# The gate block goes whole ahead of the sum of squares, and half of the key/value batch moves to the odd steps

## The chip, the cores and the metric

One core of a Trainium2 chip runs the whole program in one launch. The metric is the device time of that core in microseconds (us). Two times are told from each other by the median of several executions.

## The reference

A transformer block on 4 sequences of 256 rows and 512 channels, float32. Cut to what matters here:

```
h = layernorm(x) * (1 + ca) + sa
q, k = rope(h @ Wq.T), rope(h @ Wk.T)          # 32 heads of q, 8 of k and v, D = 128
v    = h @ Wv.T
dt = softplus(h @ Win.T + dt_bias); g = -dt * exp(A_log_bias)
# chunks of 128 rows, G = cumsum(g) in a chunk
y = (q k^T * exp(G_i - G_j), causal) @ (v dt)  +  (q exp(G)) @ state
y = y / sqrt(mean(y^2) + 1e-5) * gnorm_w
y = y * silu(h @ Wg.T)
x = x + ga * (y @ Wo.T)
x = x + gb * ffn(layernorm(x) * (1 + cb) + sb)  # silu(h Wg) * (h Wu), then Wd
```

## The kernel before

Float32 values are split into a high and a low part, and each product is three matmuls (`three_products`, L69 to L73: high x high, high x low, low x high). All engines are programmed by hand, each with its own instruction list; semaphores (`wait_ge`, `then_inc`) are the only order between them. Nothing is scheduled by a tool.

The attention runs over 8 key/value groups g, and in each over 8 steps t. Step t handles chunk c = t % 2 of sequence b = t // 2 (two chunks of 128 rows a sequence), for the four heads of the group at once. A loop holds the groups 0 to 6, and the last group is written out: its steps 0 to 3 like the loop's, its steps 4 to 7 by `tail`. Each step also computes a part of what comes later: the q projection and the gate projection of one head for half of all rows (`q_block`, `g_block`, 12 matmuls of 512 columns each), and in even steps (c = 0) the key/value projection of the next sequence, both chunks (`kv_batch`, 24 matmuls of 256 columns into the bank `ps_kv`).

TensorE's order in a step (`step`, L717 to L734): scores of the chunk (`ps_s`); `q_block`; the output product of the step before (`ps_o`, waits for `z_hi` and `z_lo`); in odd steps the transposes of k into `ps_kv` (`k_turn`, L581); y (`ps_y`, in odd steps ahead of it four products with the state, L695); in even steps the chunk's state (`ps_st`, L706); `g_block` but for its last three matmuls; the sum of squares over the head, a product of ones with `sq_hi` (L712) and with `sq_lo` (L714) into `ps_ss`; the last three gate matmuls; in even steps `kv_batch`.

What the others do around it. ScalarE (ACT), in this order: `prob_hi`; two copies of `ps_q` into `q_sin` (L778, L779); the squares of y into `work` (L877) and `sq_hi` (L878); the copy of the state or, in odd steps, of kT (L820); four exponentials of `dec`; `rms` from `ps_ss` (L888, L891); the exponential of the gate (L783); `z_hi`; two more for the gate; in even steps `v`, `v_hi` (L815, L816) and the exponential `qe` (L796) of the next sequence's decays. VectorE (DVE), in this order: `probabilities` into `work` (L1206, waits for `z_lo` of the step before and for the scores); in odd steps `rotate_k` (L996 to L1002, writes `kr`); the gate `sg` (L1029); `prob_lo`; `q_cos` (L1009); in steps 1 to 4 the high parts of the next group's weights of one head; `qT` (L1017); the sum `x` (L1035); `sq_lo` (L1223); y times gate (L1226); a low part; y times `rms` (L1233); `cap` (L1023); a low part; `z_lo`. In step 0 `wo_hi` and, at the end, `wo_lo` are split too, in step 5 the key/value weights. GpSimd (POOL): `q_sin` times the sine (L1342); in odd steps `v_lo`, `vw`, `qe`; in even steps the causal mask on the next sequence's decays (L1335, waits for ScalarE's `qe`). SyncE (SP) issues the loads of the next group's weights and decays, behind `wh_split`, `wo_split`, `kv_split` and `prob_done`, which VectorE increments.

`work` is one buffer for the probabilities, the squares, and z, so `probabilities` of a step can't start ahead of `z_lo` of the step before.

Of the kernel before, what the change touches and what calls it, by code (L numbers as in the profile page):

```python
# [1 line left out]

# [9 lines left out]
B, L, HID = 4, 256, 512  # L29
# [5 lines left out]
KT = HID // P  # L35
NT = B * L // P
CPB = L // CHUNK
# [31 lines left out]
def three_products(pe, out, w_hi, w_lo, x_hi, x_lo, first, last):  # L69

    pe.matmul(out, w_hi, x_hi, start=first, stop=False)  # L71
    pe.matmul(out, w_hi, x_lo, start=False, stop=False)  # L72
    return pe.matmul(out, w_lo, x_hi, start=False, stop=last)  # L73
# [138 lines left out]
def block_attention(nc, cst, x1, hT_hi, hT_lo, tok, modT, gnorm, ident, modrow, gT_dram,  # L212
                    x_in, cT_in, wmod_in, wq_in, wg_in, wkv_in, wo_in, win_in, rows_in,
                    gnorm_in, cst_in, wgu_in, norm_rows, raw_pair):
    with ExitStack() as ctx:
# [6 lines left out]
        def sem(name):  # L222
            return ctx.enter_context(nc.semaphore(name))
# [99 lines left out]
        kv_ready = sem("kv_ready")  # L323
# [211 lines left out]
        def _(pe):  # L535
            def q_block(g, t, first=False):

                half, j = (t // 4 + 1) % 2, t % 4
                gw = g + 1 if t >= 4 else g
                pe.wait_ge(wh_split, gw * 4 + (j + 1))  # L540
                if not first:
                    pe.wait_ge(qcos_done, g * 8 + (t + 4))
                for k in range(KT):
                    cut = slice(half * HALF, (half + 1) * HALF)
                    last = three_products(nc.tensor, ps_q[:], wq_hi[:, j, k], wq_lo[:, j, k],
                                          hT_hi[:, k, cut], hT_lo[:, k, cut], k == 0, k == KT - 1)
                last.then_inc(q_ready, 1)

            def g_block(g, t, k_from, k_to, first=False):

                half, j = (t // 4 + 1) % 2, t % 4
                if k_from == 0 and not first:
                    pe.wait_ge(sg_done, g * 8 + (t + 4))
                for k in range(k_from, k_to):
                    cut = slice(half * HALF, (half + 1) * HALF)
                    last = three_products(nc.tensor, ps_g[:], wg_hi[:, j, k], wg_lo[:, j, k],
                                          hT_hi[:, k, cut], hT_lo[:, k, cut], k == 0, k == KT - 1)
                if k_to == KT:
                    last.then_inc(g_ready, 1)

            def kv_batch(g, b):

                bn = (b + 1) % B
                gw = g + 1 if b == B - 1 else g
                pe.wait_ge(kv_split, gw + 1)
                if b >= 0:
                    pe.wait_ge(kT_done, g * 4 + (b + 1))
                for c in range(CPB):
                    cut = slice((bn * CPB + c) * P, (bn * CPB + c + 1) * P)
                    for k in range(KT):  # L570
                        last = three_products(nc.tensor, ps_kv[:, c * 2 * D:(c + 1) * 2 * D],
                                              hT_hi[:, k, cut], hT_lo[:, k, cut],
                                              wkv_hi[:, k], wkv_lo[:, k], k == 0, k == KT - 1)
                last.then_inc(kv_ready, 1)

            def k_turn(g, b):

                pe.wait_ge(kr_done, g * 4 + (b + 2))
                pe.wait_ge(v_done, g * 4 + (b + 2))
                for c in range(CPB):  # L580
                    last = nc.tensor.transpose(ps_kv[:, c * P:(c + 1) * P], kr[:, c], ident)  # L581
                last.then_inc(kt_ready, 1)

            def out_product(g, t):

                pe.wait_ge(zhi_done, g * 8 + (t + 1))
                pe.wait_ge(zlo_done, g * 8 + (t + 1))
                if t <= 1:
                    pe.wait_ge(wo_split, g + (t + 1))
                for h in range(GRP):  # L590
                    last = three_products(nc.tensor, ps_o[:], z_hi[:, h], z_lo[:, h],
                                          wo_hi[:, h], wo_lo[:, h], h == 0, h == GRP - 1)
                last.then_inc(o_ready, 1)
# [62 lines left out]
            for t in range(1, 6):  # L656
                norm.tensor_turn(pe, t)
            pe.wait_ge(norm.lo_done, CPB)
            kv_batch(0, -1)
            norm.tensor_turn(pe, 6)  # L660
            norm.tensor_turn(pe, 7)
# [13 lines left out]
            cumulative()  # L675
            q_block(0, -1)
            g_block(0, -1, 0, KT)

            def scores(g, t):

                b, c, half = t // 2, t % 2, t // 4
                pe.wait_ge(kT_done, g * 4 + (b + 1))
                pe.wait_ge(rope_done, g * 8 + (4 * half + 4))
                nc.tensor.matmul(ps_s[:].rearrange("p (h i) -> p h i", h=GRP),  # L684
                                 kT[:, b % 2, c * P:(c + 1) * P], qT[:, half, :, rows_of(t)],
                                 start=True, stop=True).then_inc(s_ready, 1)

            def y_product(g, t):

                b, c = t // 2, t % 2  # L690
                if c == 1:
                    pe.wait_ge(qe_done, g * 4 + (b + 1))
                    pe.wait_ge(state_done, g * 4 + (b + 1))
                    for h in range(GRP):
                        nc.tensor.matmul(ps_y[:, h * P:(h + 1) * P], state[:, h], qe[:, b % 2, h],  # L695
                                         start=h == 0, stop=False)
                pe.wait_ge(vlo_done, g * 4 + (b + 1))
                pe.wait_ge(plo_done, g * 8 + (t + 1))
                p_hi, p_lo = (p[:].rearrange("p h i -> p (h i)") for p in (prob_hi, prob_lo))
                three_products(nc.tensor, ps_y[:], v_hi[:, b % 2, c], v_lo[:, b % 2, c], p_hi, p_lo,  # L700
                               c == 0, True).then_inc(y_ready, 1)

            def chunk_state(g, b):

                pe.wait_ge(vw_done, g * 4 + (b + 1))
                nc.tensor.matmul(ps_st[:].rearrange("p (h e) -> p h e", h=GRP), kr[:, 0],  # L706
                                 vw[:], start=True, stop=True).then_inc(st_ready, 1)

            def square_sum(g, t):

                pe.wait_ge(sqhi_done, g * 8 + (t + 1))
                nc.tensor.matmul(ps_ss[:], ones[:], sq_hi[:], start=True, stop=False)  # L712
                pe.wait_ge(sqlo_done, g * 8 + (t + 1))
                nc.tensor.matmul(ps_ss[:], ones[:], sq_lo[:], start=False, stop=True)\  # L714
                    .then_inc(ss_ready, 1)

            def step(g, t, project, next_batch, next_group):  # L717
                b, c = t // 2, t % 2
                scores(g, t)
                if project:  # L720
                    q_block(g, t)
                out_product(g, t)
                if c == 1 and next_batch:
                    k_turn(g, b)
                y_product(g, t)
                if c == 0:
                    chunk_state(g, b)
                if project:
                    g_block(g, t, 0, KT - 1)
                square_sum(g, t)  # L730
                if project:
                    g_block(g, t, KT - 1, KT)
                if c == 0 and next_batch:
                    kv_batch(g, b)  # L734

            def tail(g, t):
                b, c = t // 2, t % 2
                if t == 4:
                    scores(g, t)
                    mod_row(GA)  # L740
                    out_product(g, t)
                if c == 1:
                    pe.wait_ge(prob_done, g * 8 + (t + 1))
                y_product(g, t)
                if c == 0:
                    chunk_state(g, b)
                    scores(g, t + 1)
                if t == 4:
                    kv_batch(g, b)
                else:  # L750
                    pe.wait_ge(lnss_done, g * 8 + t)
                if t == 5:
                    k_turn(g, b)
                    pe.wait_ge(guard, 2)
                    mod_row(CB)
                if t == 7:
                    mod_row(GB)
                square_sum(g, t)
                if t == 5:
                    scores(g, t + 1)  # L760
                if t > 4:
                    out_product(g, t)
                if t == 5:
                    mod_row(SB)
                if t == 7:
                    mod_turn(ps_late_modT, late_rows, 4)
# [989 lines left out]
```

## Time and profile before

| | us |
|---|---|
| executions | 1148.46, 1152.65, 1151.79 |
| median | 1151.79 |
| the profiled execution: time | 1148.5 |
| the profiled execution: span | 1148.5 |
| one group of eight steps in the loop | 106.6 |
| an even step | 14.1 |
| the odd steps 1, 3, 5, 7 | 13.3, 12.5, 12.4, 11.9 |

The steps are taken from one scores row (L684) to the next in the timeline. "Waited for" in square brackets behind a row is the idle time of that engine ahead of the instruction, and what released it. Matmuls overlap: what one costs in a stream is the distance between starts, not the time that its row gives.

### The profile page before, as it was taken

How to read it: one execution, taken by the hardware profiler on the slowest of the kernel's cores; microseconds unless marked ns; L12 is line 12 of the kernel's file. 1: busy time of each engine (PE TensorE's matmuls, PEld its weight loads, DVE VectorE, ACT ScalarE, POOL GpSimd, SP SyncE). 2: the span in 40 equal slices, each digit the busy share in tenths (PEclk: the TensorE clock that was granted, in tenths of full speed). 3: DMA queues.
4: the chain of work that ended last, by engine and by line, in shares of the span. 5: the costliest groups of instructions: out<-in, count | busy, mean ns of one | idle time of the engine just before them, and what ended most of it. 6: DMA issues, size and time to landing. Idle time of an engine off the chain costs nothing. (4 is left out here: it accounts for less than half of the span.)

```text
span 1148.5 us, 14892 instructions
## 1 busy us (share of the span) xinstructions
PE 1076.9 (94%) x4936; PEld 835.7 (73%) x4936; DVE 848.1 (74%) x1432; ACT 612.4 (53%) x1257; POOL 328.7 (29%) x227
## 2 busy tenths in 40 slices
PE   4879999999999999999999999999999869999898
PEld 2657778777777777777777777777776348888676
DVE  5768887988788788879877887888787786434311
ACT  3445666666566666666666656666665434222300
POOL 3423333333433333333333333333332630000000
PEclk9989999999999999999999999999999989999899
DMA  6121301220131013112201310131031422111011
GB/s 216 56 69 56 116 22 37 73 73 18 37 110 37 18 37 120 35 41 76 74 18 37 110 37 18 37 110 37 21 105 32 173 88 78 55 37 55 28 37 37
DMA packets 37466, 70.90 MB, mean 62 GB/s; under 512 B 2937, under 2 KB 19577, under 8 KB 35521
## 3 DMA queue, kind: packets, MB, share of 16 engines
q1 hardware_dynamic: 36720, 70.16, 19.3%
q10 hardware_dynamic: 720, 0.43, 0.1%
q8 instruction: 14, 0.23, 0.1%
q14 instruction: 12, 0.09, 0.0%
HBM read 68.33 MB, written 2.24 MB: 61 GB/s over the span
## 5 line engine op out<-in xcount | busy, mean ns | idle before, releaser
L1342 POOL TENSOR_TENSOR q_sin<-q_sin,cst 128x512 f32<-128x512 f32 x64 | 92.3, 1443 | 295.5 <-ACT q_sin L779 295.4
L1335 POOL TENSOR_TENSOR dec<-dec,future 128x1024 f32<-128x1024 f32 x31 | 78.1, 2519 | 268.2 <-ACT qe L796 268.2
L71 PE MATMUL ps_q<-hT_hi,wq_hi 128*128 128x512 f32 x256 | 125.7, 491 | 2.8 <-DVE q_cos L1009 2.3
L71 PE MATMUL ps_gt<-hT_hi,wg_hi 128*128 128x512 f32 x256 | 114.6, 448 | 3.6 <-DVE sg L1029 3.6
L877 ACT ACTIVATE work<-ps_y 128x512 f32<-128x512 f32 x64 | 38.3, 598 | 146.5 <-PE ps_y L73 144.0
L71 PE MATMUL ps_o<-wo_hi,z_hi 128*128 128x512 f32 x260 | 103.8, 399 | 3.1 <-DVE z_lo L66 3.1
L73 PE MATMUL ps_o<-wo_hi,z_lo 128*128 128x512 f32 x260 | 103.1, 397 | 0.0
L72 PE MATMUL ps_o<-wo_lo,z_hi 128*128 128x512 f32 x260 | 102.7, 395 | 0.0
L73 PE MATMUL ps_gt<-hT_hi,wg_lo 128*128 128x512 f32 x256 | 102.2, 399 | 0.0
L72 PE MATMUL ps_gt<-hT_lo,wg_hi 128*128 128x512 f32 x256 | 102.0, 399 | 0.0
L73 PE MATMUL ps_q<-hT_hi,wq_lo 128*128 128x512 f32 x256 | 101.5, 397 | 0.0
L72 PE MATMUL ps_q<-hT_lo,wq_hi 128*128 128x512 f32 x256 | 101.0, 395 | 0.0
L1233 DVE TENSOR_TENSOR work<-work,rms 128x512 f32<-128x512 f32 x64 | 45.3, 708 | 58.2 <-ACT rms L891 58.2
L806 ACT ACTIVATE dec<-dec,scal 128x128 f32<-128x128 f32 x256 | 82.0, 407 | 1.4 <-DVE scal L987 1.4
L1206 DVE SCALAR_TENSOR_TENSOR work<-ps_s,scal,dec 128x128 f32<-128x128 f32 x240 | 67.6, 345 | 19.8 <-DVE z_lo L66 11.2
L1017 DVE TENSOR_TENSOR qT<-q_cos,q_sin 128x512 f32<-128x512 f32 x64 | 65.6, 1025 | 17.7 <-POOL q_sin L1342 17.7
L888 ACT ACTIVATE rms<-ps_ss,eps_col 128x512 f32<-128x512 f32 x64 | 44.0, 688 | 55.6 <-PE ps_ss L714 55.6
L71 PE MATMUL ps_kv<-wkv_hi,hT_hi 128*128 128x256 f32 x256 | 73.4, 287 | 0.0
L73 PE MATMUL ps_kv<-wkv_hi,hT_lo 128*128 128x256 f32 x256 | 72.8, 284 | 0.0
L72 PE MATMUL ps_kv<-wkv_lo,hT_hi 128*128 128x256 f32 x256 | 72.6, 284 | 0.0
L66 DVE TENSOR_TENSOR sq_lo<-work,sq_hi 128x512 fp32r<-128x512 f32 x64 | 61.7, 964 | 13.9 <-ACT sq_hi L878 13.9
L684 PE MATMUL ps_s<-qT,kT 128*128 128x512 f32 x128 | 65.5, 593 | 3.5 <-DVE qT L1017 3.5
(249 smaller groups left out, 2817.0 us busy)
## 6 DMA issues: line engine op xcount, KB each, us to landing
dec<-gT_dram SPq DMA_DIRECT2D x32, 512.0 KB, 5.5
raw_q<-wq_in SPq DMA_DIRECT2D x32, 256.0 KB, 2.7
raw_g<-wg_in SPq DMA_DIRECT2D x32, 256.0 KB, 3.0
raw_o<-wo_in SPq DMA_DIRECT2D x8, 1024.0 KB, 7.1
raw_pair<-wkv_in SPq DMA_DIRECT2D x8, 512.0 KB, 4.7
raw_pair<-wgu_in SPq DMA_DIRECT2D x6, 512.0 KB, 3.4
raw_gu<-wgu_in SPq DMA_DIRECT2D x5, 512.0 KB, 3.4
qT<-wmod_in SPq DMA_DIRECT2D x2, 1024.0 KB, 7.3
```

The source lines that it names most:

```text
L66: return engine.tensor_tensor(lo, full, hi.bitcast(F32), ALU.subtract)
L71: pe.matmul(out, w_hi, x_hi, start=first, stop=False)
L72: pe.matmul(out, w_hi, x_lo, start=False, stop=False)
L73: return pe.matmul(out, w_lo, x_hi, start=False, stop=last)
L684: nc.tensor.matmul(ps_s[:].rearrange("p (h i) -> p h i", h=GRP), kT[:, b % 2, c * P:(c + 1) * P], qT[:, half, :, rows_of(t)], start=True, ...
L806: last = nc.scalar.activation(cell, cell, ACT.Exp, bias=scal[:, bn * CPB + c, 0, h:h + 1])
L888: nc.scalar.activation(rms[:], ps_ss[:], ACT.Ln, bias=eps_col[:], scale=1.0 / D)\
L1017: nc.vector.tensor_tensor(qT[:, half, j], q_cos[:], q_sin[:], ALU.add)\
L1206: last = nc.vector.scalar_tensor_tensor(dest[:, h], ps_s[:, h * P:(h + 1) * P], scal[:, t, 1, h:h + 1], dec[:, b % 2, h, c], ALU.mult, ALU ...
L1233: nc.vector.tensor_tensor(z[:], z[:], rms[:].rearrange("p (h i) -> p h i", h=GRP), ALU.mult).then_inc(z_done, 1)
L1335: nc.gpsimd.tensor_tensor(cells, cells, future[:].unsqueeze(1).broadcast_to([P, GRP * CPB, CHUNK]), ALU.add).then_inc(mask_done, 1)
L1342: nc.gpsimd.tensor_tensor(q2, q2, sinT, ALU.mult).then_inc(qsin_done, 1)
```

## The change

On TensorE alone, the order of the same instructions. All twelve gate matmuls go ahead of the sum of squares. The key/value batch of a sequence is cut by chunk: chunk 0 is projected behind the sum of squares in the odd step before (with a wait for the copy of kT of that step, `kT_done`, because `k_turn` has used the same part of `ps_kv`), chunk 1 in the even step. Step 5 (b == B - 2) has no such half, because the next group's key/value weights are being split in it; step 6 keeps both chunks. The half for step 0 of the first group is put ahead of the loop.

```
-            def kv_batch(g, b):
+            def kv_batch(g, b, chunks=range(CPB)):
                 bn = (b + 1) % B
                 gw = g + 1 if b == B - 1 else g
                 pe.wait_ge(kv_split, gw + 1)
                 if b >= 0:
                     pe.wait_ge(kT_done, g * 4 + (b + 1))
-                for c in range(CPB):
+                for c in chunks:
...
-                last.then_inc(kv_ready, 1)
+                if CPB - 1 in chunks:
+                    last.then_inc(kv_ready, 1)
...
             g_block(0, -1, 0, KT)
+            kv_batch(0, 0, range(1))
...
                 if project:
-                    g_block(g, t, 0, KT - 1)
+                    g_block(g, t, 0, KT)
                 square_sum(g, t)
-                if project:
-                    g_block(g, t, KT - 1, KT)
+                if c == 1 and next_batch and b != B - 2:
+                    kv_batch(g if b < B - 1 else g + 1, (b + 1) % B, range(1))
                 if c == 0 and next_batch:
-                    kv_batch(g, b)
+                    kv_batch(g, b, range(1, CPB) if b < B - 1 else range(CPB))
...
                 if t == 4:
-                    kv_batch(g, b)
+                    kv_batch(g, b, range(1, CPB))
```

Two places of TensorE's list show what moves. Line numbers of the changed file are 15 to 17 lower (L54 to L56 are L71 to L73, L697 and L699 are the sum of squares, L669 the scores).

Before, step 0 of a group (even), from the end of the first nine gate matmuls (`ps_gt`) over the sum of squares (`ps_ss`) to the first of the 24 key/value matmuls (`ps_kv`):

```order
L73 MATMUL ps_gt<-hT_hi,wg_lo 128x512
L712 MATMUL ps_ss<-sq_hi,ones_r 128x512 [waits sqhi_done]
L714 MATMUL ps_ss<-sq_lo,ones_r 128x512 [waits sqlo_done]
L71 MATMUL ps_gt<-hT_hi,wg_hi 128x512
L72 MATMUL ps_gt<-hT_lo,wg_hi 128x512
L73 MATMUL ps_gt<-hT_hi,wg_lo 128x512
L71 MATMUL ps_kv<-wkv_hi,hT_hi 128x256 [waits kT_done,kv_split]
```

The same place after the change:

```order
L54 MATMUL ps_gt<-hT_hi,wg_hi 128x512
L55 MATMUL ps_gt<-hT_lo,wg_hi 128x512
L56 MATMUL ps_gt<-hT_hi,wg_lo 128x512
L697 MATMUL ps_ss<-sq_hi,ones_r 128x512 [waits sqhi_done]
L699 MATMUL ps_ss<-sq_lo,ones_r 128x512 [waits sqlo_done]
L54 MATMUL ps_kv<-wkv_hi,hT_hi 128x256 [waits kT_done,kv_split]
```

Here the last three gate matmuls have gone ahead of the sum, and 12 matmuls of `ps_kv` follow where 24 did. Before, step 1 (odd), from the last matmul of y to the scores (`ps_s`) of step 2 the list has nine of `ps_gt`, the sum, three of `ps_gt` and the scores; its end:

```order
L712 MATMUL ps_ss<-sq_hi,ones_r 128x512 [waits sqhi_done]
L714 MATMUL ps_ss<-sq_lo,ones_r 128x512 [waits sqlo_done]
L71 MATMUL ps_gt<-hT_hi,wg_hi 128x512
L72 MATMUL ps_gt<-hT_lo,wg_hi 128x512
L73 MATMUL ps_gt<-hT_hi,wg_lo 128x512
L684 MATMUL ps_s<-qT,kT 128x512 [waits rope_done,kT_done]
```

The same place after the change, the sum with the first of the 12 key/value matmuls that now stand between it and the scores:

```order
L56 MATMUL ps_gt<-hT_hi,wg_lo 128x512
L697 MATMUL ps_ss<-sq_hi,ones_r 128x512 [waits sqhi_done]
L699 MATMUL ps_ss<-sq_lo,ones_r 128x512 [waits sqlo_done]
L54 MATMUL ps_kv<-wkv_hi,hT_hi 128x256 [waits kT_done,kv_split]
L55 MATMUL ps_kv<-wkv_lo,hT_hi 128x256
```

The gate block is whole ahead of the sum, and a half batch has come in behind it, in an odd step, where there was none.

## Rows read from the trace of the kernel before

**Rows 1.** The page: busy time by engine, and TensorE's clock in 40 slices.

```profile
PE 1076.9 (94%) x4936; PEld 835.7 (73%) x4936; DVE 848.1 (74%) x1432; ACT 612.4 (53%) x1257; POOL 328.7 (29%) x227
...
PEclk9989999999999999999999999999999989999899
```

**Rows 2.** Waits of TensorE in 80 to 826 us: total, times, longest.

```profile
PE ps_ss L714 <- DVE sq_lo L66: 19.8, 21, 1.6
PE ps_s L684 <- DVE qT L1017: 3.5, 1, 3.5
```

**Rows 3.** Timeline of TensorE, one group: start, duration (us), what.

```profile
517.37 0.39 PE L714 MATMUL ps_ss<-sq_lo,ones_r 128*128 128x512 f32 x1
...
518.29 0.28 PE L71 MATMUL ps_kv<-wkv_hi,hT_hi 128*128 128x256 f32 x1
...
521.16 1.02 PE L684 MATMUL ps_s<-qT,kT 128*128 128x512 f32 x2
...
527.62 0.38 PE L581 MATMUL ps_kv<-cst,kr 128*128 128x128 f32 x2
...
531.52 0.40 PE L712 MATMUL ps_ss<-sq_hi,ones_r 128*128 128x512 f32 x1
533.45 0.50 PE L714 MATMUL ps_ss<-sq_lo,ones_r 128*128 128x512 f32 x1 [1.53 <-DVE sq_lo L66]
...
544.80 0.39 PE L714 MATMUL ps_ss<-sq_lo,ones_r 128*128 128x512 f32 x1
...
560.02 0.50 PE L714 MATMUL ps_ss<-sq_lo,ones_r 128*128 128x512 f32 x1 [0.70 <-DVE sq_lo L66]
...
571.41 0.39 PE L714 MATMUL ps_ss<-sq_lo,ones_r 128*128 128x512 f32 x1
...
586.53 0.50 PE L714 MATMUL ps_ss<-sq_lo,ones_r 128*128 128x512 f32 x1 [0.57 <-DVE sq_lo L66]
```

**Rows 4.** Timeline of VectorE, steps 0 and 1 of that group.

```profile
519.25 0.69 DVE L1233 TENSOR_TENSOR work<-work,rms 128x512 f32<-128x512 f32 x1 [0.84 <-ACT rms L891]
...
520.64 0.69 DVE L66 TENSOR_TENSOR z_lo<-work,z_hi 128x512 fp32r<-128x512 f32 x1 [0.37 <-ACT z_hi L899]
...
525.34 0.74 DVE L1002 TENSOR_TENSOR kr<-q_cos 128x256 f32<-128x256 f32 x1
...
532.72 0.68 DVE L66 TENSOR_TENSOR sq_lo<-work,sq_hi 128x512 fp32r<-128x512 f32 x1
```

**Rows 5.** Timeline of ScalarE, VectorE and GpSimd around steps 3 and 5.

```profile
549.65 0.63 ACT L796 ACTIVATE qe<-dec 128x512 f32<-128x512 f32 x1
549.71 1.13 DVE L1206 SCALAR_TENSOR_TENSOR work<-ps_s,scal,dec 128x128 f32<-128x128 f32 x4 [0.80 <-DVE z_lo L66]
550.36 2.39 POOL L1335 TENSOR_TENSOR dec<-dec,future 128x1024 f32<-128x1024 f32 x1 [8.28 <-ACT qe L796]
...
551.60 1.45 DVE L1002 TENSOR_TENSOR kr<-q_cos 128x256 f32<-128x256 f32 x1
...
576.97 2.39 POOL L1335 TENSOR_TENSOR dec<-dec,future 128x1024 f32<-128x1024 f32 x1 [8.32 <-ACT qe L796]
...
578.20 1.45 DVE L1002 TENSOR_TENSOR kr<-q_cos 128x256 f32<-128x256 f32 x1
...
584.78 1.70 DVE L66 TENSOR_TENSOR sq_lo<-work,sq_hi 128x512 fp32r<-128x512 f32 x1 [0.41 <-ACT sq_hi L878]
```

**Rows 6.** Timeline: step 6 of that group, and step 4 of the last group.

```profile
589.91 0.69 DVE L66 TENSOR_TENSOR z_lo<-work,z_hi 128x512 fp32r<-128x512 f32 x1 [0.36 <-ACT z_hi L899]
...
591.21 0.39 PE L71 MATMUL ps_o<-wo_hi,z_hi 128*128 128x512 f32 x1
...
891.94 0.38 ACT L815 ACTIVATE v<-ps_kv 128x256 f32<-128x256 f32 x1 [2.96 <-PE ps_kv L73]
...
896.23 0.47 PE L71 MATMUL ps_y<-prob_hi,v_hi 128*128 128x512 f32 x1 [2.17 <-DVE prob_lo L66]
```

**Rows 7.** Busy time: us; PE, PEld, DVE, ACT, POOL; PEclk; DMA share; GB/s.

```profile
879.00:950.00 71.00, 54.01 (x200) 30.37 (x199) 57.24 (x99) 29.28 (x68) 29.02 (x19) 0.90 0.36 132
```

## Prediction

> **What bounds the kernel now.** I read the page first: TensorE is busy in 94% of the span, VectorE in 74%, ScalarE in 53%, GpSimd in 29%, and TensorE's clock is at its upper level, 2.4 GHz, through the eight key/value groups [rows 1]. So TensorE sets the time and only its idle stretches can be won. The list of waits, cut to the eight-group loop, has two entries for TensorE: 19.8 us in 21 waits of the second half of the sum of squares (L714) for `sq_lo`, which VectorE writes, and one of 3.5 us ahead of the first scores [rows 2]. The change goes for the first entry.
>
> The timeline gives the place. A group is eight steps, t = 0 to 7, and the group from 507.02 us stands for all, because the steps of one t last the same in every group. I call X(t) the start of L714 in step t: 517.37, 533.45, 544.80, 560.02, 571.41 and 586.53 for t = 0 to 5 [rows 3]; what changes in steps 6 and 7 is small. The 21 waits are those of t = 1, 3 and 5 in seven groups; even steps never wait. In t = 1 the first half of the sum starts at 531.52, and a matmul of this shape takes 0.23 us in the stream (four of them from 517.37 to 518.29), so L714 could go at 531.75 and goes at 533.45: 1.70 us lost.
>
> What is VectorE doing until then? Its rows are the heart of the matter [rows 4]. At 519.25 it gets `rms` of step **0**, normalises, writes `z_lo`, and from 520.64 on it has no idle time at all until `sq_lo` of step **1** ends at 533.40. So the wait in t = 1 isn't set by the product y of that step, on which a few more matmuls of cover would help. It is the end of a chain of 16.03 us that begins with the sum of squares of the even step before. L714 of t = 1 comes 16.08 us after X(0) whatever TensorE does between, as long as TensorE does less than that. The same distance is 15.22 us for t = 3 and 15.12 for t = 5. The list counts no wait in t = 7, which has no weights to split.
>
> **The change part by part.** No instruction is added or removed, and there are as many matmuls, loads and semaphore increments as before. Three things move on TensorE.
>
> First, the three last gate matmuls go from behind the sum to ahead of it, in all 60 projecting steps: 0.69 us, three of the four between 517.37 and 518.29 [rows 3]. Seen between one X and the next this is worth nothing: the three leave the start of the interval and come in at its end. The sum comes 0.7 us later after y, and 0.7 us less stands between it and the next product. ScalarE takes the gate (L783) after `rms` in its own order, so the earlier gate block gives nothing, and the later `rms` costs only what the next two points count.
>
> Second, twelve of the 24 key/value matmuls go from the even step to the odd step ahead of it. 24 take 518.29 to 521.16 = 2.87 us, twelve take 1.43 us. Between X(t) and X(t+1) TensorE's work so changes:
> - from X(0) to X(1), X(2) to X(3), X(4) to X(5): 1.43 us **less**
> - from X(1) to X(2), X(3) to X(4), X(7) to the next X(0): 1.43 us **more**
> - from X(5) to X(6) and X(6) to X(7): the same, since t = 5 gets no half and t = 6 keeps all 24.
>
> The two kinds don't cancel. In the intervals that end in an even step TensorE is never idle, so 1.43 us more is 1.43 us later. In those that end in t = 1, 3, 5 the chain sets the length: TensorE has 531.75 - 517.37 = 14.38 us of work before and 12.95 after (t = 3 and 5 have the same instructions), against 16.08, 15.22 and 15.12 us. The work taken out was cover for the chain. The waits should grow from 1.70, 0.84 and 0.74 us to 3.13, 2.27 and 2.17 us, and part of them should move forward to the transposes of k (L581) and to y, which wait for `kr` and `prob_lo` of the same chain (in t = 1 `kr` is there 8.71 us after X(0), 526.08 less 517.37, and TensorE would ask for it at 527.62 - 517.37 - 0.69 - 1.43 = 8.13). That is 3 x 1.43 = 4.3 us a group. Over the program the longer intervals are seven of the third kind and eight of each of the others, 23 x 1.43 = 32.9 us.
>
> What can the earlier work give back? Scores of an odd step now start 1.43 + 0.69 = 2.1 us earlier after X. In t = 1 VectorE doesn't wait for them (it is at `wo_lo`), so they give nothing. In t = 3 it waits 0.80 us ahead of 549.71, and in t = 5 as long [rows 5]. The row names `z_lo`, but that had ended when the wait began, and the scores are the only other thing of that moment; t = 5 waits another 0.41 us for `sq_hi` at 584.78. These could shorten the chain by 0.80 and 1.21 us. But the row behind stands against it: `kr` (two inputs from SBUF) starts at 551.60 and takes 1.45 us, ending at 553.05, 0.30 us after GpSimd's mask ends (550.36 + 2.39 = 552.75). In t = 5 it ends at 579.65, 0.29 after the mask's 579.36. Where nothing holds it up for long, in t = 1, it takes 0.74 us [rows 4]. The mask follows the exponential `qe` on ScalarE (549.65 + 0.63), which runs back to back from `z_hi`, with nothing from TensorE in it that is late [rows 5]. If `kr` is held until the mask ends, starting it 0.8 us sooner gives nothing, and the chain behind it is the same. So the bounds are 0 and 0.80 us for t = 3, 0 and 1.21 for t = 5, and I take 0.1 each, because `kr`'s end follows the mask in both rows.
>
> The Trainium skill, "SBUF — State Buffer", section "Who interferes with whom", says the same of this pair: a VectorE instruction with two SBUF inputs and a GpSimd one that reads SBUF exclude each other, and the second fully blocks. The two rows agree. By that rule alone the gain of t = 3 and 5 is zero, and by a rule of free overlap the sum would be 13 us lower.
>
> Third, the small ones. In t = 7 nothing was waited for, and nothing is gained. In t = 6 the output product started at 591.21 and its `z_lo` was done at 590.60 [rows 6]; 0.69 earlier, after a late X(5) with nothing behind it, it waits 0.1: +0.7 us in seven groups. The half batch ahead of the loop runs in the 3.5 us wait for `qT` ahead of the first scores [rows 2]: -1.4 us. In the last group t = 3 splits no weights, and the 1.43 us taken out ahead of it are in part not missed: 0 to -1.43, I take -0.5. At t = 4 of the last group ScalarE waits 2.96 us for the batch, the mask is behind it, `prob_lo` behind that, and TensorE waits 2.17 us for it [rows 6]; a batch that is 1.43 us shorter gives up to that: -1.4 us. The new wait of the half batch for `kT_done` costs nothing: that copy is the next thing ScalarE does behind the squares for which L712 waits anyway, and VectorE's `sq_lo` is still to come then. SyncE's loads wait for semaphores of VectorE alone and move with the chain; no queue is passed.
>
> Sum: 32.9 - 0.8 - 0.7 (t = 3, t = 5) + 0.7 (t = 6) - 1.4 - 0.5 - 1.4 = 28.8 us. On the profiled execution, whose time is its span of 1148.5 us, that is 1177.3 us. That execution is the fastest of the three, the median is 3.3 us above it, on which the sum gives 1180.6. I say 1178, since the unknown parts of the sum can only give time back.
>
> **The rivals.**
> - *The chain gives way.* Everything as above, but the earlier scores and `sq_hi` shorten the chain in full: -0.80 x 8 and -1.21 x 7, so 32.9 - 6.4 - 8.5 - 2.6 = 15.4 us, 1164 to 1167. It holds if `kr` doesn't end with the mask.
> - *The three matmuls cover the wait (faster).* If `sq_lo` followed y of its own step, L714 would have 0.69 us more ahead of it in t = 1, 3, 5. The waits of 1.53, 0.70 and 0.57 us in the profile's rows fall by 0.69, 0.69 and 0.57 us, seven times: 13.7 us, which gives 1135 to 1138 us. It decides when VectorE has idle time ahead of `sq_lo` larger than 1.43 us, the cover taken. For it: `sq_lo` of t = 5 does wait 0.41 us for ScalarE. Against: t = 1 has none from 520.64 to 533.40, and t = 3 none from 549.71.
> - *The clock falls.* TensorE's granted clock has a mean of 0.90 in 879 to 950 us, where it waits often, against the upper level all through the loop [rows 1, 7]. Now t = 1 has 3.1 us of idle time in about 8 us. One stretch of a few us at 1.2 GHz doubles its matmuls: if 2 us of work a group goes at half the clock where nothing waits, that is another 16 us, 1194.
> - *It cancels.* The chain's relief plus a reordering of VectorE and GpSimd that favours VectorE gives all back: 1149 to 1157.
>
> The Trainium skill, "TensorE: Matmul & The Clock Gate", section "HAM oscillation — how this bites in real kernels", warns of waits between groups of matmuls letting the clock go down. In the loop of this trace waits of 1.7 us didn't; no run here shows 3.1 us in pieces.
>
> **How the numbers follow.** The forecast has 0.65 (1170 to 1186), the yielding chain 0.13 (1161 to 1170), the clock 0.05 (over 1188), cancelling 0.07, faster 0.10. The range that leaves out the last three is 1161 to 1188. About 0.5% (6 us) is what can be told from no change. Slower by more: 0.65 + 0.13 + 0.05 and a bit of cancelling, 0.84. Same: 0.06. Faster: 0.10.
>
> **What would show it.** In the changed kernel's profile: X(0) to X(1) stays at 16.1 us, X(2) to X(3) and X(4) to X(5) at 15.1 to 15.3; X(1) to X(2), X(3) to X(4) and X(7) to X(0) are 12.8 us and more, 1.43 us longer than before. TensorE's waits in t = 1, 3, 5 sum to some 7.5 us a group (3.3 before), with some at L581 and y. `kr` ends 0.3 us after the mask. The group lasts 110.5 us instead of 106.6. The prediction is wrong if X(2) to X(3) shrinks to 14.4 (the chain gives way), or if VectorE's rows show idle time ahead of `sq_lo` in t = 1.

## The result, and the profile after

The changed kernel takes 1169.01 us (median of 4 executions, 1167.53 to 1172.24), the kernel before 1150.28 (median of 4 by then). The ratio is 1.0173, with a 95% interval of 1.0157 to 1.019: slower. The profiled execution has a span of 1165.7 us, 17.2 above that of before.

Line numbers of the changed kernel are 15 to 17 lower than before: L699 is L714, L669 the scores, L565 the transposes of k, L987 `kr`, L1320 the mask. Its page, with the lines that answer to [rows 1]:

```profile
PE 1089.0 (93%) x4936; PEld 835.8 (72%) x4936; DVE 865.3 (74%) x1432; ACT 610.2 (52%) x1257; POOL 327.8 (28%) x227
...
PEclk9999999999999999999999999999999988999999
```

The same 4936 matmuls, and no fall of the clock in the loop. The page alone can't say where 17 us went. The list of waits of TensorE in 80 to 845 us can (total, times, longest), beside [rows 2]:

```profile
PE ps_ss L699 <- DVE sq_lo L49: 12.8, 21, 1.0
PE ps_y L54 <- DVE prob_lo L49: 11.5, 21, 0.8
PE ps_o L54 <- DVE wo_lo L49: 5.1, 7, 0.7
```

The wait ahead of L714 looks better, 12.8 us for 19.8. But two have come in that weren't there, and the three together are 29.4 us. A fourth, the 3.5 us ahead of the first scores, is gone, since the half batch now runs there. A single row of this list that shrinks is no proof of a gain: the wait has moved forward on the same chain. The timeline of one group of the loop (start, duration in us), steps 0 to 3, shows it beside [rows 3, 4]:

```profile
528.10 0.39 PE L699 MATMUL ps_ss<-sq_lo,ones_r 128*128 128x512 f32 x1
529.77 1.02 PE L669 MATMUL ps_s<-qT,kT 128*128 128x512 f32 x2
...
533.67 2.86 POOL L1320 TENSOR_TENSOR dec<-dec,future 128x1024 f32<-128x1024 f32 x1 [9.90 <-ACT qe L781]
536.07 0.75 DVE L987 TENSOR_TENSOR kr<-q_cos 128x256 f32<-128x256 f32 x1
537.21 0.38 PE L565 MATMUL ps_kv<-cst,kr 128*128 128x128 f32 x2
539.24 0.47 PE L54 MATMUL ps_y<-prob_hi,v_hi 128*128 128x512 f32 x1 [0.75 <-DVE prob_lo L49]
543.44 0.68 DVE L49 TENSOR_TENSOR sq_lo<-work,sq_hi 128x512 fp32r<-128x512 f32 x1
544.17 0.49 PE L699 MATMUL ps_ss<-sq_lo,ones_r 128*128 128x512 f32 x1 [0.96 <-DVE sq_lo L49]
...
556.99 0.39 PE L699 MATMUL ps_ss<-sq_lo,ones_r 128*128 128x512 f32 x1
...
562.56 2.40 POOL L1320 TENSOR_TENSOR dec<-dec,future 128x1024 f32<-128x1024 f32 x1 [9.75 <-ACT qe L781]
563.02 2.22 DVE L987 TENSOR_TENSOR kr<-q_cos 128x256 f32<-128x256 f32 x1
564.92 1.46 POOL L1327 TENSOR_TENSOR q_sin<-q_sin,cst 128x512 f32<-128x512 f32 x1
565.83 1.10 DVE L49 TENSOR_TENSOR prob_lo<-work,prob_hi 128x512 fp32r<-128x512 f32 x1
...
571.63 0.50 PE L699 MATMUL ps_ss<-sq_lo,ones_r 128*128 128x512 f32 x1 [0.59 <-DVE sq_lo L49]
```

Read it from X to X. X(0) to X(1) is 544.17 - 528.10 = 16.07 us, as before (16.08), though the scores come 1.67 us after X(0) and not 3.79. X(1) to X(2) is 12.82 us, 1.47 more than before. In step 3 `kr` is issued 0.77 us earlier after X(2) than before, takes 2.22 us and not 1.45, and ends at 565.24, 8.25 us after X(2), to the hundredth where it ended before. X(2) to X(3) is still 0.58 us shorter, 14.64 for 15.22.

All intervals, in us, of the group that starts nearest to 510 us, of each kernel of this study. They come from the L714 rows of each timeline. The other six loop groups agree within 0.1 us, with these exceptions: in group 0 the first interval is 18.88 us in e5, 15.42 in e6, 14.40 in e7 and 14.69 in e9; in group 6 the last one is 11.5 in e1, e6 and e7; and step 4 of e4, see there.

| kernel | 0 to 1 | 1 to 2 | 2 to 3 | 3 to 4 | 4 to 5 | 5 to 6 | 6 to 7 | 7 to 0 | sum |
|---|---|---|---|---|---|---|---|---|---|
| before | 16.08 | 11.35 | 15.22 | 11.39 | 15.12 | 11.36 | 14.65 | 11.39 | 106.6 |
| changed | 16.07 | 12.82 | 14.64 | 12.81 | 14.35 | 11.68 | 14.39 | 12.70 | 109.5 |
| e1 gate part alone | 16.07 | 11.84 | 14.79 | 11.82 | 14.51 | 11.67 | 14.39 | 11.68 | 106.8 |
| e2 half batch alone | 16.06 | 12.80 | 14.63 | 12.81 | 14.35 | 11.38 | 14.66 | 12.81 | 109.5 |
| e3 three quarters | 16.07 | 13.54 | 14.62 | 13.53 | 14.35 | 11.67 | 14.40 | 13.42 | 111.6 |
| e4 sine late | 16.07 | 12.81 | 15.54 | 14.39 | 14.16 | 11.75 | 14.41 | 12.70 | 111.8 |
| e5 decay early | 17.71 | 12.71 | 13.85 | 12.81 | 13.55 | 11.66 | 14.39 | 12.72 | 109.4 |
| e6 gate first, wo_lo early | 16.00 | 11.84 | 14.78 | 11.81 | 14.49 | 11.69 | 14.39 | 11.70 | 106.7 |
| e7 that and decay early | 15.21 | 11.82 | 14.39 | 11.72 | 14.40 | 11.55 | 14.40 | 11.68 | 105.2 |
| e8 e7 with the half batch | 14.62 | 12.80 | 13.83 | 12.81 | 13.56 | 11.67 | 14.39 | 12.72 | 106.4 |
| e9 e7 without the gate part | 15.02 | 11.35 | 14.79 | 11.35 | 14.66 | 11.38 | 14.39 | 11.23 | 104.2 |

Of the 17.2 us between the two profiled executions, the seven loop groups have 20.2 (766.4 us from the first scores of group 0 to those of group 7, 746.2 before), the start gives back 1.6 (first scores at 79.05 and not 80.61), and the last group with the rest of the program gives back 1.4.

### The profile page after: what moved, and what is told of

Read it like the earlier page. It is cut to its first block and busy times, and to the rows that moved or that the text cites. A ratio compares the mean times of both kernels' runs of the same rounds, so it can differ in the third digit from the quotient of the medians.

```text
span 1165.7 us, 14916 instructions
## 1 busy us (share of the span) xinstructions
PE 1089.0 (93%) x4936; PEld 835.8 (72%) x4936; DVE 865.3 (74%) x1432; ACT 610.2 (52%) x1257; POOL 327.8 (28%) x227
## 5 line engine op out<-in xcount | busy, mean ns | idle before, releaser
L1320 POOL TENSOR_TENSOR dec<-dec,future 128x1024 f32<-128x1024 f32 x31 | 78.0, 2517 | 302.1 <-ACT qe L781 302.1
L1327 POOL TENSOR_TENSOR q_sin<-q_sin,cst 128x512 f32<-128x512 f32 x64 | 84.9, 1327 | 276.0 <-ACT q_sin L764 275.9
L54 PE MATMUL ps_q<-hT_hi,wq_hi 128*128 128x512 f32 x256 | 126.8, 495 | 2.9 <-DVE q_cos L994 2.4
L54 PE MATMUL ps_gt<-hT_hi,wg_hi 128*128 128x512 f32 x256 | 114.3, 446 | 2.1 <-DVE sg L1014 2.1
L54 PE MATMUL ps_o<-wo_hi,z_hi 128*128 128x512 f32 x260 | 105.4, 405 | 9.3 <-DVE wo_lo L49 5.9
L56 PE MATMUL ps_o<-wo_hi,z_lo 128*128 128x512 f32 x260 | 103.0, 396 | 0.0
L56 PE MATMUL ps_q<-hT_hi,wq_lo 128*128 128x512 f32 x256 | 102.1, 399 | 0.0
L56 PE MATMUL ps_gt<-hT_hi,wg_lo 128*128 128x512 f32 x256 | 102.0, 398 | 0.0
L1002 DVE TENSOR_TENSOR qT<-q_cos,q_sin 128x512 f32<-128x512 f32 x64 | 64.7, 1011 | 12.7 <-POOL q_sin L1327 12.4
L54 PE MATMUL ps_kv<-wkv_hi,hT_hi 128*128 128x256 f32 x256 | 73.8, 288 | 0.0
L56 PE MATMUL ps_kv<-wkv_hi,hT_lo 128*128 128x256 f32 x256 | 72.8, 284 | 0.0
L54 PEld LDWEIGHTS ps_o<-wo_hi,z_hi 128*128 128x128 f32 x260 | 49.2, 189 | 27.2 <-issue 8.6
L54 PEld LDWEIGHTS ps_q<-hT_hi,wq_hi 128*128 128x128 f32 x256 | 48.4, 189 | 27.0 <-issue 17.4
```

What stands on the lines that cost most here:

```text
L1002: nc.vector.tensor_tensor(qT[:, half, j], q_cos[:], q_sin[:], ALU.add)\
L1320: nc.gpsimd.tensor_tensor(cells, cells, future[:].unsqueeze(1).broadcast_to([P, GRP * CPB, CHUNK]), ALU.add).then_inc(mask_done, 1)
L1327: nc.gpsimd.tensor_tensor(q2, q2, sinT, ALU.mult).then_inc(qsin_done, 1)
```

## The experiments

**e1, the gate part alone.** The kernel before, with this edit:

```
-                if project:
-                    g_block(g, t, 0, KT - 1)
-                square_sum(g, t)
-                if project:
-                    g_block(g, t, KT - 1, KT)
+                if project:
+                    g_block(g, t, 0, KT)
+                square_sum(g, t)
```

> The kernel before with only the first part of the change: all twelve gate matmuls ahead of the sum of squares, the key/value batch left whole in the even step. X(t) is the start of the second half of the sum of squares in step t. Theory (a chain on VectorE from the sum of the even step sets L714 of the odd step): the part is nearly neutral. X(0) to X(1) stays 16.1 us. X(2) to X(3) and X(4) to X(5) shorten from 15.2 and 15.1 to about 14.6 and 14.4, since scores come 0.69 us earlier. Each even step pays 0.3 us, because the output product now catches up with z_lo, so X(1) to X(2), X(3) to X(4), X(5) to X(6), X(7) to X(0) grow from 11.4 to 11.7. Sum: -0.3 us a group, ratio 0.995 to 1.001. Rival (the three matmuls cover the wait of the same step): the waits of t = 1, 3, 5 fall by 0.69, 0.69, 0.57 us, 13.7 us in all, ratio 0.988.

Measured: 1147.88 us, ratio 0.9986 (0.9974 to 0.9998), inside what was expected. X(0) to X(1) has not moved; the rival's 0.988 is out. X(2) to X(3) and X(4) to X(5) are 14.79 and 14.51 us, 0.1 to 0.2 us longer than expected, and so a group is 0.2 us longer than before where 0.3 less was said. TensorE's waits in the loop:

```profile
PE ps_ss L714 <- DVE sq_lo L66: 8.3, 14, 1.0
PE ps_o L71 <- DVE z_lo L66: 2.8, 14, 0.2
PE ps_y L71 <- DVE prob_lo L66: 2.2, 7, 0.3
```

The wait for `sq_lo` is down from 19.8 us to 8.3, which looks like the 13.7 us that the rival promised. But a group lasts 106.8 us and not 106.6, so seven last some 1.4 us more than before, where the rival wants 13.7 less: the even-to-odd intervals get shorter, but the odd-to-even ones pay 0.3 to 0.5 us each (11.35 to 11.84), part of it for `z_lo`. The small gain in the total lies outside the loop, mostly in the last group and after it (316.7 us from the first scores of group 7 to the end, 321.7 before). Its cause is open.

**e2, the half batch alone.** The changed kernel with the lines of the gate block as before.

> The kernel before with only the second part: half of the key/value batch in the odd steps, the gate block as before (nine matmuls, the sum, three matmuls). Theory: this part has the whole loss. X(0) to X(1) 16.1 us, the intervals that end in steps 2, 4 and the next 0 grow by 1.43 us to 12.8, X(2) to X(3) and X(4) to X(5) shorten to about 14.6 and 14.4, and step 6 does not pay the 0.3 us. +2.8 us a group, ratio 1.014 to 1.019. Rival (the two parts only lose together, or the gate part has the loss): under 1.008.

Measured: 1170.65 us, ratio 1.0176 (1.0153 to 1.02), inside what was expected, and so are the intervals. The loss is in this part, all of it. It shows too that the 0.3 us of steps 6 and 7 belong to the gate part: without it 5 to 6 is 11.38 and 6 to 7 is 14.66, as before.

**e3, more of the batch.** `kv_batch` takes a list of (chunk, k) parts; the first six of eight go to the odd step:

```
+            EARLY_PARTS, LATE_PARTS = ALL[:6], ALL[6:]
...
-                    kv_batch(g if b < B - 1 else g + 1, (b + 1) % B, range(1))
+                    kv_batch(g if b < B - 1 else g + 1, (b + 1) % B, EARLY_PARTS)
```

> The changed kernel with 18 of the 24 key/value matmuls in the odd step before (chunk 0 and the first half of chunk 1) and 6 left in the even step. Theory: the cover taken out of the intervals that end in steps 1, 3, 5 was all that stood between TensorE and the chain, so each matmul moved costs its full time in the three intervals that end in steps 2, 4, 0: 6 x 0.12 = 0.72 us more than in the changed kernel, 12.8 to 13.5 us, three times a group, and X(0) to X(1) stays 16.1. 23 x 0.72 = 16 us above the changed kernel: 1183 to 1187 us, ratio to the kernel before 1.030 to 1.033. Rival (the loss comes from the fact of a split, its semaphores or the write into the bank, not from the amount): as the changed kernel, 1.017.

Measured: 1186.74 us, ratio 1.0326 (1.0296 to 1.0356), 17.7 us above the changed kernel, as expected. The three intervals grew by 0.72 us each, what six matmuls cost, and X(0) to X(1) stays at 16.07. The price goes with the amount moved.

**e4, the sine late.** In the changed kernel GpSimd waits before it multiplies `q_sin`:

```
                 if project:
+                    if t in (3, 5):
+                        pool.wait_ge(plo_done, g * 8 + (t + 1))
                     rotate_q_sin(g, t)
```

> The changed kernel, where GpSimd in steps 3 and 5 waits for prob_lo before it multiplies q_sin by the sine (L1327), so that it takes that place behind prob_lo again, as in the kernel before. Theory: X(2) to X(3) and X(4) to X(5) shrank from 15.2 and 15.1 to 14.6 and 14.35 us in the changed kernel because this multiplication starts 1 us earlier and so gets its SBUF time while VectorE is in gate; with the wait they go back to 15.1 to 15.6, about 0.7 us each, 10 us in all, 1177 to 1181 us, ratio 1.024 to 1.028. Rival (the chain shortened because kr, the probabilities or sq_hi come earlier): no change or 0.2 us each, 1169 to 1172.

Measured: 1183.25 us, ratio 1.0285 (1.0261 to 1.0309), 2 us above what was expected. Right for step 3, wrong for step 5. X(2) to X(3) is back at 15.54 us. X(4) to X(5) is 14.16, shorter still, though the sine starts at 9.67 us after X(4) and not at 7.93. Two rows of VectorE and GpSimd in that step (X(4) = 595.97) show what took its place:

```profile
609.15 0.93 DVE L49 TENSOR_TENSOR sq_lo<-work,sq_hi 128x512 fp32r<-128x512 f32 x1
609.49 1.73 POOL L1345 TENSOR_TENSOR qe<-qe,qT 128x512 f32<-128x512 f32 x1
```

With GpSimd that late, `sq_lo` starts ahead of GpSimd's `qe` and no longer ends behind it. So the total agrees with the expectation only in part for its reason: over the seven groups step 3 gives 6.3 us, step 5 takes off 1.3, and 6.4 us are a surprise in step 4 of four of the seven groups (14.4 us where the others have 12.8). Another 4.7 us of the difference between the two profiled executions lie outside the loop, 2.8 of them ahead of the first scores, and aren't explained. Stretches around X(3) = 581.58 of one of the four: length, busy time of PE, PEld, DVE, ACT, POOL, granted clock, DMA:

```profile
566.00:581.60 15.60, 13.65 (x67) 10.44 (x65) 13.57 (x21) 8.88 (x19) 7.03 (x5) 1.00 0.20 68
581.60:585.00 3.40, 3.40 (x15) 2.84 (x16) 2.67 (x5) 2.51 (x5) 0.00 (x0) 0.61 0.00 0
585.00:588.50 3.50, 3.50 (x14) 2.51 (x13) 3.22 (x8) 1.71 (x3) 0.00 (x0) 0.89 0.54 151
```

and the rows there:

```profile
579.28 0.40 PE L697 MATMUL ps_ss<-sq_hi,ones_r 128*128 128x512 f32 x1
581.58 0.50 PE L699 MATMUL ps_ss<-sq_lo,ones_r 128*128 128x512 f32 x1 [1.90 <-DVE sq_lo L49]
584.11 1.84 PE L669 MATMUL ps_s<-qT,kT 128*128 128x512 f32 x2
```

Behind a wait of 1.9 us in one piece the granted clock has a mean of 0.61 from 581.60 to 585.00, so TensorE runs at 1.2 GHz for most of that stretch: X to scores takes 2.53 us instead of 1.67, and the interval 1.6 us more. The other three groups have the same wait and no fall. That is the rival on the clock, at the price of 1.6 us a fall, in another kernel than the one it was made for.

**e5, the decays early.** In the changed kernel ScalarE takes `qe` right behind `z_hi`:

```
                 split_z_hi(g, t)
+                if c == 0:
+                    exp_g(g, b)
                 sigmoid(g, t)
                 if c == 0:
                     copy_v(g, b)
-                    exp_g(g, b)
```

> The changed kernel, where ScalarE in even steps takes the exponential of the next decays (L781) right behind z_hi and not behind the gate's two and the copies of v; GpSimd's mask, which waits for it, so starts 1.7 us earlier, at 3.9 us after X(even) and not at 5.6. Theory (the mask holds kr, in steps 3 and 5 until 8.25 us after X whenever kr is issued): kr ends at about 6.9 us, X(2) to X(3) and X(4) to X(5) shorten from 14.6 and 14.35 to 13.3 to 13.9 us; TensorE's own work there is 12.95. In step 0 to 1 the mask meets wo_lo: if wo_lo goes first, X(0) to X(1) stays 16.1 and the kernel takes 1152 to 1160 us; if the mask goes first, it grows to 18.3, and the whole is 1168 to 1175. Rival (kr's end at 8.25 us has another reason, such as the copies of v or a rate of VectorE): kr stays at 8.2 us, X(2) to X(3) stays at 14.6.

Measured: 1170.81 us, ratio 1.0176 (1.0152 to 1.02), inside the range that was given for the case that the mask goes first. Step 3, X(2) = 560.47:

```profile
564.32 2.55 POOL L1321 TENSOR_TENSOR dec<-dec,future 128x1024 f32<-128x1024 f32 x1 [8.03 <-ACT qe L781]
...
566.86 0.43 DVE L988 TENSOR_TENSOR kr<-q_cos 128x256 f32<-128x256 f32 x1
```

Out of the mask's way `kr` takes 0.43 us, not 1.45 or 2.22, and ends 6.82 us after X (6.9 expected, 8.25 before). X(2) to X(3) is 13.85 and X(4) to X(5) 13.55. Where the mask and `wo_lo` meet, in step 0 to 1, the mask was first:

```profile
533.90 2.38 POOL L1321 TENSOR_TENSOR dec<-dec,future 128x1024 f32<-128x1024 f32 x1 [8.14 <-ACT qe L781]
533.94 4.48 DVE L49 TENSOR_TENSOR wo_lo<-raw_o,wo_hi 128x2048 fp32r<-128x2048 f32 x1
538.48 0.50 PE L54 MATMUL ps_o<-wo_hi,z_hi 128*128 128x512 f32 x1 [2.92 <-DVE wo_lo L49]
```

0.04 us decide: `wo_lo` takes 4.48 us, 2.29 before, and ends 2.1 us behind the mask. TensorE waits 2.92 us for it, and its clock falls in every group behind that (a mean of 0.62 from 538.50 to 543.00). X(0) to X(1) went up by 1.64 us (18.3 us were put at this case, 17.71 measured), and gain and loss cancel.

**e6, wo_lo early, on e1.** VectorE splits `wo_lo` in step 0 ahead of the normalisation:

```
                 if t == 0:
                     split_o_hi(g)
+                    split_o_lo(g)
                 normed_z(g, t)
...
-                if t == 0:
-                    split_o_lo(g)
```

> The kernel with the gate block whole ahead of the sum (key/value batch whole in the even step), and VectorE's wo_lo (2.29 us) taken in step 0 ahead of the normalisation, where VectorE waits 1.5 us for rms, and not between z_lo and the probabilities of step 1. Theory (the chain from X(0) sets X(1)): normalisation comes 0.7 us later, 2.2 us leave the chain, X(0) to X(1) falls from 16.07 to between 14.6 and 15.2 us, 0.9 to 1.5 us a group, 1137 to 1141 us, ratio to the kernel before 0.989 to 0.992. Rival (the wait in step 1 belongs to that step's own work): no change against that kernel's 1147.9.

Measured: 1146.52 us, ratio 0.9972 (0.996 to 0.9983), 1.4 us from e1, where 7 to 11 were expected. The expectation fell, by the rows of step 0 to 1, X(0) = 516.57:

```profile
517.22 2.29 DVE L66 TENSOR_TENSOR wo_lo<-raw_o,wo_hi 128x2048 fp32r<-128x2048 f32 x1
519.43 0.68 DVE L1231 TENSOR_TENSOR work<-work,rms 128x512 f32<-128x512 f32 x1
...
523.11 2.42 POOL L1332 TENSOR_TENSOR dec<-dec,future 128x1024 f32<-128x1024 f32 x1 [9.86 <-ACT qe L794]
523.42 2.38 DVE L1000 TENSOR_TENSOR kr<-q_cos 128x256 f32<-128x256 f32 x1
...
532.57 0.50 PE L714 MATMUL ps_ss<-sq_lo,ones_r 128*128 128x512 f32 x1 [0.96 <-DVE sq_lo L66]
```

VectorE issues `kr` 6.85 us after X(0), 1.1 us sooner than before, and then stands 2 us for the mask. The mask hangs on `z_hi`, which has become 1.0 us later (3.58 us after X(0), 2.61 in e1) because the normalisation has. So "busy without a gap" was no proof that VectorE's own work sets the chain: a long row may be a wait inside an instruction.

**e7, both edits on e1.**

> Both edits of the other two on the kernel with the gate block first: wo_lo ahead of the normalisation, and the exponential of the decays ahead of the gate's. Theory: the chains of all four odd steps get shorter than TensorE's own work of 14.4 us, so X(even) to X(odd) is 14.4 to 14.6 everywhere; -1.6 us in step 1, -0.4 in step 3, -0.1 in step 5 against the gate-first kernel, 15 us in all, 1132 to 1136 us, ratio 0.984 to 0.988. Rival (the earlier mask blocks z_lo or the probabilities' low part): above 1140.

Measured: 1134.66 us, ratio 0.9869 (0.9846 to 0.9892), inside what was expected. Alone, one had given nothing on the changed kernel (e5) and the other nothing on e1 (e6); together they give 13.2 us against e1. Steps 3, 5 and 7 are at TensorE's own 14.4 us, step 1 at 15.21 (14.6 expected, since the normalisation behind `wo_lo` is late).

**e8, the half batch on e7.** The changed kernel with both edits.

> The changed kernel (gate block first and half of the key/value batch in odd steps) with both edits of the run before: wo_lo ahead of the normalisation of step 0, the exponential of the decays ahead of the gate's. It differs from e7 by the half batch alone. Theory (cover taken from the intervals that end in steps 1, 3, 5): the even-to-odd intervals are chain-bound at about 15.2, 13.8 and 13.6 us, where TensorE's own work would be 12.95, and the odd-to-even ones grow by 1.0 to 1.4 us: +2.7 us a group against e7, 1152 to 1158 us, ratio to the kernel before 1.001 to 1.006. Rival (with shorter chains the half batch costs nothing): as e7, 1135.

Measured: 1145.97 us, ratio 0.9969 (0.9954 to 0.9984). The sign is as expected, the half batch costs 11.3 us against e7, but it is less than the 17 to 23 us that were said, and the total lies below the range of 1152 to 1158; (106.4 - 105.2) x 7 = 8.4 of them are in the seven groups. X(0) to X(1) is 14.62 us where 15.2 were put in. The rows of VectorE say where the 0.6 us are: here `wo_lo` starts 0.09 us after X(0) and the normalisation at 2.29, in e7 0.67 and 2.88. X(0) stands later against VectorE's queue, so less of `wo_lo` is left ahead of the normalisation, and everything behind it on the chain comes the same 0.6 us sooner.

**e9, both edits on the kernel before.** TensorE's order is untouched.

> The kernel before (nine gate matmuls, the sum, three; batch whole) with the same two edits of VectorE and ScalarE, TensorE's order untouched. It differs from e7 by the gate block alone. Theory: the odd-to-even intervals are 11.4 us, not 11.55 to 11.8, since the output product doesn't catch up with z_lo; the even-to-odd ones are about 15.5, 14.6, 14.5, 14.65 against 15.2, 14.4, 14.4, 14.4. Sum -0.5 us a group against e7, 1129 to 1134 us, ratio 0.983 to 0.986. Rival (gate first is worth its place once the chains are short): above 1136.

Measured: 1131.82 us, ratio 0.9847 (0.9824 to 0.9871), inside what was expected, the fastest of all, 18 us below the kernel before. `kr` of step 0 to 1 is free of the mask, X(0) = 507.25:

```profile
512.53 2.42 POOL L1335 TENSOR_TENSOR dec<-dec,future 128x1024 f32<-128x1024 f32 x1 [8.12 <-ACT qe L796]
515.07 0.42 DVE L1003 TENSOR_TENSOR kr<-q_cos 128x256 f32<-128x256 f32 x1
...
522.27 0.50 PE L714 MATMUL ps_ss<-sq_lo,ones_r 128*128 128x512 f32 x1 [0.49 <-DVE sq_lo L66]
```

The gain came from ScalarE and VectorE, in the chain that TensorE waits for, and not from TensorE's order. The 2.8 us between e7 and e9 are near the edge of what the runs tell apart. In the seven groups of the profiled executions e9 is 6 us shorter, and ahead of them and behind them e7 is 4 us shorter. Which share of the 18 us each of the two edits has is not separated: neither ran alone on the kernel before.

## Why the prediction was right, and where its sum was off

**The core held.** "The work taken out was cover for the chain": X(0) to X(1) was said to stay at 16.08 and is 16.07. The three odd-to-even intervals were said to grow by 1.43 us each, and grew by 1.47, 1.42 and 1.31, 4.20 us a group for 4.29. e2 puts the loss on the half batch, e3 makes it grow by the matmul, e1 shows the gate part at nearly nothing in the loop. The rival in which three more matmuls cover the wait is out by e1.

**Two of its own signs came out between the forecast and its rival.** X(2) to X(3) was to stay at 15.1 to 15.3, and 14.4 was to show that the chain gives way: 14.64 was measured, and 14.35 for X(4) to X(5). The waits of t = 1, 3, 5, taken as interval less 12.95 us of own work, are 6.2 us a group and not 7.5, and a group lasts 109.5 us and not 110.5 (the terms of the sum give 110.8, so that figure didn't follow from them).

**The sum was 28.8 us, the profiled execution shows 17.2.** The terms, in the order of what they were off by:
- Step 5: 0.1 us a group was taken out of the bounds 0 and 1.21; it gave 0.77, so 4.7 us over seven groups. "The chain behind it is the same" failed. `kr` did end at 8.25 us after X(4) as said. But VectorE isn't alone on the chain behind it: GpSimd's own list is there too, the sine, `v_lo`, `vw` and `qe`, and `sq_lo` stands until that `qe` ends. Before (X(4) = 571.41; `sq_lo` is in [rows 5]):

```profile
580.34 1.73 POOL L1342 TENSOR_TENSOR q_sin<-q_sin,cst 128x512 f32<-128x512 f32 x1 [0.98 <-ACT q_sin L779]
...
584.63 1.29 POOL L1360 TENSOR_TENSOR qe<-qe,qT 128x512 f32<-128x512 f32 x1
```

  and changed (X(4) = 584.44):

```profile
592.37 1.46 POOL L1327 TENSOR_TENSOR q_sin<-q_sin,cst 128x512 f32<-128x512 f32 x1
...
596.44 1.74 POOL L1345 TENSOR_TENSOR qe<-qe,qT 128x512 f32<-128x512 f32 x1
...
597.55 1.19 DVE L49 TENSOR_TENSOR sq_lo<-work,sq_hi 128x512 fp32r<-128x512 f32 x1
```

  `qe` ends 14.51 us after X(4) before and 13.74 now, and `sq_lo` ends 0.56 us behind it both times: 0.77 us. The sine had waited for the copies of `ps_q`, so for TensorE's `q_block`, and that block now comes 2.1 us earlier. In e4 the sine is late again and the interval short all the same, but there `sq_lo` slips in ahead of `qe`; so e4 shows a second way to the same gain and neither proves nor excludes this one, which rests on rows.
- Step 3: 0.1 was taken of 0 to 0.80; it gave 0.58, 3.4 us. `kr` stayed, as said. GpSimd's sine starts at 7.93 us after X(2), right behind the mask, and not at 8.92. It costs `prob_lo` 0.4 us (1.10 for 0.68), but `vw` is over before `qT` starts, so `qT` takes 0.68 us and not 1.52, and `qe`, which waits for `qT`, ends 0.58 us sooner. `sq_lo` ends 0.55 us behind `qe` in the kernel before, in the changed one and in e4. e4 took the early sine back, and the interval went to 15.54: here the cause is shown.
- Last group and what follows: +1.0 was in the sum (2 x 1.43 less 0.5 and 1.4), -1.4 was measured. Right were X(1) to X(2) (+1.4) and X(2) to X(3) (-0.6). X(3) to X(5) was put at nothing on balance and is 1.4 shorter, 0.9 of it in step 5: `z_lo` takes 0.69 us and not 1.59, since it now starts ahead of a GpSimd instruction (L424) and not behind its start. The stretches ahead of X(0) and behind X(7), also put at nothing, are 0.8 shorter together, and that is open.
- Steps 6 and 7: 0.32 lost for 0.1 said (the output product starts 0.46 us behind the matmul ahead of it, 0.15 us behind the end of `z_lo`, and the next one 0.30 us behind it, where 0.23 is usual), 0.26 gained in step 7 where 0 was said. They cancel.
- The 0.12 us less in step 7 to 0 (1.31 for 1.43) and the start (1.6 for 1.4) are small.

**The description of the chain was half right.** It said that VectorE has no idle time from `z_lo` to `sq_lo` of the next step, and took its own work as the length. It also took the `kr` of t = 1, 0.74 us, for one that nothing holds up for long; 0.43 us is what `kr` takes when free (e5), and the mask of t = 1 ended at 525.80, 0.28 us ahead of it. e5 and e6 show that the chain leaves VectorE: `rms`, normalisation, `z_hi`, ScalarE's gate and v, `qe`, GpSimd's mask, and back to VectorE at `kr`. For X(0) to X(1) it made no difference, since both start at X(even) and TensorE held up neither. In steps 3 and 5 it did, by the 0.58 and 0.77 us above. For mending the kernel it made all: e6, built on the first reading, gave nothing, and e7 and e9 13 us and more.

**The clock** didn't fall in the loop of the changed kernel (granted 1.00 in 80 to 845 us). Step 1 is 3.1 us longer there than TensorE's own work, and its three waits are shown with 0.7 to 1.0 us. It fell in e4 and e5, behind 1.9 and 2.9 us in one piece.

**The range and the number.** 1169.0 us lies in the range, but not in the band of the forecast (1170 to 1186, chance 0.65): it is 1 us under it, in that of the chain that gives way (1161 to 1170, chance 0.13), and 9 us under the 1178 that was named. The relief in steps 3 and 5 is 9.5 us (0.58 and 0.77, seven times), where the forecast has 1.5 and that rival 14.9. The three longer intervals and the unmoved X(0) to X(1) were foreseen for their reason; how much comes back in steps 3 and 5 was not, and that the total still fell in the range is owed to its width.

Open: why the whole batch with the gate part ahead (e1, e6, e7) makes the last group and the rest of the program up to 5 us shorter. The rows place most of it in the last group: X(4) to X(5) is 8.87 us there (12.96 before), X(5) to X(6) 12.7 to 14.3 (11.76).

## What to carry to other kernels

Work that the bounding engine does between two points of a loop of waits is cover for the chain between these points; moving it to the neighbouring interval costs its full time there and gives nothing back here (X(0) to X(1)), however evenly it then lies, except what it moves within the chain itself (0.58 and 0.77 us in steps 3 and 5). Measure from the same instruction of one step to that of the next and compare with the engine's own work in between, rather than add up the list of waits, where one row may fall by half (e1) without a gain. And an engine that looks busy without a gap may be standing in an instruction: compare the duration of one instruction between steps (`kr`: 0.43, 0.75, 1.45, 2.22 us) before its work is called the bound.

## What the runs showed of the hardware

VectorE instructions with two SBUF inputs didn't share with GpSimd's here, they stood until the other ended: `kr` (0.43 us free) took 2.22 us under a mask, and `wo_lo` (2.29 us) 4.48 when the mask had started 0.04 us before. Where VectorE stood waiting at the end of a GpSimd instruction it went ahead of GpSimd's next: the sine behind the mask is shown with 1.46 us when `kr` was waiting (step 3) and with 1.27 when it wasn't (step 1). The Trainium skill, "SBUF — State Buffer", section "Who interferes with whom", has the first, that such a pair excludes each other, and these rows agree. That earlier scores could still help by changing who is first was not drawn from it. The clock fell behind one wait of 1.9 us in four groups of seven, each time at the price of 1.6 us, and behind one of 2.9 us in every group; 3.1 us in pieces with matmuls between them (and 3.8 in e3, none longer than 1.5) did nothing. That the pieces are what matters is the likely reading of these rows, though no run varies it alone.
